# A softmax over heads on one Trainium2 core: six of eight heads copied by ScalarE, two by a DMA of the SyncE queue

## The chip, the core and the metric

The kernel runs on 1 core of one Trainium2 chip. The metric is the device time of the whole program in microseconds, from one launch. The engines that are named below are TensorE (PE), VectorE (DVE), ScalarE (ACT), GpSimd (POOL) and SyncE (SP, which only issues DMAs here).

## The reference

A layer normalisation stands before each of four residual blocks: banded attention, a mixture of experts, attention with its softmax over the heads, and the mixture of experts again, on x of shape (4, 1024, 128). The change lies in the third block:

```python
q = (x @ Wq.T + bq).reshape(B, S, H, D)      # B 4, S 1024, H 16, D 8
k = (x @ Wk.T + bk).reshape(B, S, H, D)
v = (x @ Wv.T + bv).reshape(B, S, H, D)
scores = jnp.einsum('bqnd,bknd->bnqk', q, k) / jnp.sqrt(jnp.float32(D))
attn = jax.nn.softmax(scores, axis=1)        # axis 1 is the head
out = jnp.einsum('bnqk,bknd->bnqd', attn, v)
```

For each pair of a query and a key the 16 exponentials of the heads are added up, and each is divided by that sum.

## The kernel before, in words

The block is the function `head_softmax_attention`. A chunk is 128 queries (4 batches of 8, so 32 chunks), a unit is a chunk against 128 keys (`kt` 0 to 7 in a chunk, so 256 units). In a unit the scores stand with the keys on the 128 partitions, 16 heads x 128 queries along the row; they are made in two halves h of 64 queries each (h0, h1), since each half of all heads fills two PSUM banks of `score`.

For each unit and half: PE makes the scores (`scores_of`, L893); DVE takes the maximum over the heads, negated (`largest`, L1118); PE adds it to the scores (`take_maximum`, L915); ACT takes the exponential into `ex` (L1072), which is a ring of RING = 6 units in SBUF. Only then can PE overwrite that half of `score`.

The sum over 16 heads goes in steps. ACT copies heads 0 to 7 of `ex` into `half` (`copy_heads`, L1035), a ring of SUMS = 4 units. GpSimd issues a DMA that adds heads 8 to 15 onto them (`add_halves`, L847, an accumulating DMA), and when that has landed GpSimd adds four heads to four others (`add_quarters`, L853). PE adds the last four with an identity matrix (`denominator_of`, L925) into `den`. ACT takes the logarithm and exp of its negative, twice (L1041, L1044, L1046). DVE weighs heads 0 to 9 (`weigh`, L1125), GpSimd heads 10 to 15 (`weigh_rest`, L859), and PE multiplies by the values (`attend`, L908), which waits for GpSimd's part only ahead of the 11th head.

The order on each engine is written out by hand. In unit u:
- PE: `take_maximum` h0 of u; `scores_of` h1 of u; `denominator_of` u-4; `scores_of` h0 of u+1; `take_maximum` h1 of u; `attend` u-5; and with even kt a projection or the output product (`ahead`).
- DVE: `largest` h1 of u; `largest` h0 of u+1; `weigh` u-4; and in most units one small operation.
- ACT: exp h0 of u; copy of u-1; the three small ones of u-4; exp h1 of u; with kt 1 and 3 a copy of a projection, with kt 5 that of the output.
- GpSimd, in step u: `add_halves` u-1; `weigh_rest` u-4; `add_quarters` u-2.
- SyncE: once per chunk the queries of the next chunk go to HBM (L804) and come back in another layout in four pieces (L809); in the first three batches so do the keys of the next batch (L814, L816).

Of the kernel before, what the change touches and what calls it, by code (L numbers as in the profile page):

```python
# [21 lines left out]
B, S, E = 4, 1024, 128  # L22
T = B * S
NT = T // P
BT = S // P
# [34 lines left out]
ONE = 1  # L60
# [655 lines left out]
def head_softmax_attention(nc, c, x, mv, ht, q_dram, k_dram, k_first, zero_f16, zero_f32):  # L716
# [6 lines left out]
    NQ = S // P  # L723
    LAST = B * NQ - 1
    LAG, RING, SUMS = 4, 6, 4
    ON_DVE = 10
    BY_DMA = 0
    ALL = B * NQ * BT
    SLABS = range(NH // 4)
    HALVES = S // BLK  # L730
    READS_Q = GH
    xnT, HB, GR, vs = ht.xnT, ht.HB, ht.GR, ht.vs
    with Mem(nc, "head") as m:
# [4 lines left out]
        parts_q, parts_k = m.sb("parts_q", [P, SLOTS, P], F16), m.sb("parts_k", [P, SLOTS, P], F16)  # L738
        parts_first = m.sb("parts_first", [P, HALVES, SLOTS, BLK], F16)
        shift = m.sb("shift", [P, 2, QS], BF16)  # L740
        ex = m.sb("ex", [P, RING, NH, P])
        half = m.sb("half", [P, SUMS, NH // 2, P])
# [6 lines left out]
        k_ready, k_high, k_low = m.sem("k_ready", "pe"), m.sem("k_high", "act"), m.sem("k_low", "dve")  # L749
        q_written, q_placed = m.sem("q_written", "sp"), m.sem("q_placed", "sp")  # L750
        k_written, k_placed = m.sem("k_written", "sp"), m.sem("k_placed", "sp")
        v_ready, v_done = m.sem("v_ready", "pe"), m.sem("v_done", "dve")
        score_ready, shift_ready, shifted = m.sem("score_ready", "pe"), m.sem("shift_ready", "dve"), m.sem("shifted", "pe")
        ex_ready, den_ready = m.sem("ex_ready", "act"), m.sem("den_ready", "pe", 1)
# [3 lines left out]
        av_done, outT_ready = m.sem("av_done", "pe", RING - 1), m.sem("outT_ready", "act")  # L758
        out_ready, added = m.sem("out_ready", "pe"), m.sem("added", "dve")
        summed = [m.sem(f"summed{i}") for i in range(2)]  # L760
        std, rstd = m.sb("std", [P, NT]), m.sb("rstd", [P, NT])
        xn = m.sb("xn", [P, 2, TB, E])
        rstd_chain, std_ready = m.sem("rstd_chain", "dve"), m.sem("std_ready", "act")
# [5 lines left out]
        def exps(unit, h):  # L769

            return 3 * unit + 2 if h == 1 else max(3 * unit, 1)

        def copies(unit):

            return 3 * unit + (4 if unit < ALL - 1 else 3)
# [22 lines left out]
        @block.sync  # L798
        def _(sp):
            m.start(sp, "sp")  # L800

            def place_q(n):
                sp.wait_ge(q_low, ONE + n + 1)
                sp.dma_start(q_dram[:, :, :], parts_q[:, :, :]).then_inc(q_written, 16)  # L804
                sp.wait_ge(q_written, ONE + (n + 1) * 16)
                by_row = q_dram.rearrange("(g r) s c -> (r s) g c", g=NG)
                for n4 in range(GH):
                    rows = slice(n4 * SLOTS * D, (n4 + 1) * SLOTS * D)
                    sp.dma_start(HB[rows, n % 2, n4:NH:GH, :], by_row[rows, :, :]).then_inc(q_placed, 16)  # L809
                sp.wait_ge(q_placed, ONE + (n + 1) * (READS_Q * 16))  # L810

            def place_k(n, buf, kt):
                sp.wait_ge(k_low, ONE + n + 1)
                sp.dma_start(k_dram[:, :, :], parts_k[:, :, :]).then_inc(k_written, 16)  # L814
                sp.wait_ge(k_written, ONE + (n + 1) * 16)
                sp.dma_start(GR[:, buf, :, kt * P:(kt + 1) * P], k_dram.rearrange("(g r) s c -> (r s) g c", g=NG)).then_inc(k_placed, 16)  # L816
                sp.wait_ge(k_placed, ONE + (n + 1) * 16)

            def clear_values(buf):
                sp.dma_start(vs[:, buf * BT:(buf + 1) * BT, :].rearrange("p t s -> p (t s)"), zero_f32.partition_broadcast(P)).then_inc(v_zeroed, 16)  # L820

            sp.dma_start(HB[:, :, :, :].rearrange("p a n q -> p (a n q)"), zero_f16.partition_broadcast(KROWS)).then_inc(q_zeroed, 16)
            clear_values(0)
            for i in range(HALVES):
                sp.wait_ge(k_low, ONE + i + 1)
                sp.dma_start(k_first[i], parts_first[:, i, :, :]).then_inc(k_written, 16)
            sp.wait_ge(k_written, ONE + HALVES * 16)
            for i in range(HALVES):
                sp.dma_start(GR[:, 0, :, i * BLK:(i + 1) * BLK], k_first[i].rearrange("(g r) s c -> (r s) g c", g=NG)).then_inc(k_placed, 16)
            sp.wait_ge(q_zeroed, ONE + 16)  # L830
            place_q(0)
            clear_values(1)
            for b in range(B):
                for q in range(NQ):
                    if b * NQ + q < LAST:
                        place_q(b * NQ + q + 1)
                    if b < B - 1:
                        place_k(HALVES + b * NQ + q, (b + 1) % 2, q)

        @block.gpsimd  # L840
        def _(pool):
            m.start(pool, "pool")

            def add_halves(unit):

                pool.wait_ge(ex_ready, ONE + copies(unit))
                pool.dma_start(half[:, unit % SUMS, :, :], ex[:, unit % RING, 8:16, :], accum_op=ALU.add).then_inc(summed[unit % 2], 16)  # L847

            def add_quarters(unit):

                pool.wait_ge(summed[unit % 2], (unit // 2 + 1) * 16)
                hf = half[:, unit % SUMS, :, :]
                pool.tensor_tensor(hf[:, 0:4, :], hf[:, 0:4, :], hf[:, 4:8, :], ALU.add).then_inc(quarter_ready, 1)  # L853

            def weigh_rest(unit):

                pool.wait_ge(copy_ready, ONE + unit + 1)
                e = ex[:, unit % RING, ON_DVE:NH, :]
                pool.tensor_tensor(e, e, recip[:, unit % 2, :][:, None, :].broadcast_to([P, NH - ON_DVE, P]),  # L859
                                   ALU.mult).then_inc(rest_ready, 1)  # L860

            for step in range(ALL + 1):
                if step > 0:
                    add_halves(step - 1)
                if step >= LAG:
                    weigh_rest(step - LAG)
                if step > 1:
                    add_quarters(step - 2)
            add_quarters(ALL - 1)
            for unit in range(ALL + 1 - LAG, ALL):  # L870
                weigh_rest(unit)
# [145 lines left out]
        def _(act):  # L1017
# [14 lines left out]
            def copy_heads(unit):  # L1032

                act.wait_ge(ex_ready, ONE + exps(unit, 1))
                act.activation(half[:, unit % SUMS, BY_DMA:8, :], ex[:, unit % RING, BY_DMA:8, :], ACT.Copy).then_inc(ex_ready, 1)  # L1035

# [651 lines left out]
def build(nc, drams, x_dram, out):  # L1688
    with ExitStack() as ctx:
        c = {n: ctx.enter_context(nc.sbuf_tensor(f"c_{n}", s, dt)) for n, (s, dt) in SHAPES.items()}  # L1690
        x = ctx.enter_context(nc.sbuf_tensor("x_tokens", [P, NT, E], F32))
        for n in WEIGHTS:
            c[n] = ctx.enter_context(nc.sbuf_tensor(f"c_{n}", [P, WEIGHTS[n], 2, P], F16))
        for att in ("a_", "b_"):
            c[att + "bias"] = ctx.enter_context(nc.sbuf_tensor(f"c_{att}bias", [P, 2], F32))
        c["a_out"] = ctx.enter_context(nc.sbuf_tensor("c_a_out", [P, E], F32))

        mv = ctx.enter_context(nc.sbuf_tensor("moments", [P, NT, 2], F32))
        w_dram = nc.dram_tensor("pair_weights", [NPAIR, 2, T], F32).ap()

        q_dram = nc.dram_tensor("a_queries", [P, SLOTS, QCOLS], F16).ap()
        k_dram = nc.dram_tensor("a_keys", [P, SLOTS, KCOLS], F16).ap()
        v_dram = nc.dram_tensor("a_values", [LEFT + T + VTAIL, E], F32).ap()
        with Mem(nc, "att_a") as m:
            bt = BandTensors(m)
            banded_attention(nc, c, x, mv, bt, q_dram, k_dram, v_dram, x_dram, drams)
        feed_forward(nc, "ffn1", c, x, mv, w_dram, True)
        bq_dram = nc.dram_tensor("b_queries", [P, SLOTS, P], F16).ap()
        bk_dram = nc.dram_tensor("b_keys", [P, SLOTS, P], F16).ap()
        zero_f16, zero_f32 = drams["zero_f16"], drams["zero_f32"][0:BT * (NH + 1) * VSLOT]  # L1710
        bk_first = nc.dram_tensor("b_keys_first", [S // BLK, P, SLOTS, BLK], F16).ap()
        with Mem(nc, "att_b") as m:
            ht = HeadTensors(m)
            head_softmax_attention(nc, c, x, mv, ht, bq_dram, bk_dram, bk_first, zero_f16, zero_f32)
        feed_forward(nc, "ffn2", c, x, mv, w_dram, False, out)
# [72 lines left out]
```

## Time and profile before

| | |
|---|---|
| median of 3 runs | 1930.84 us (1929.66 to 1932.56) |
| the profiled execution | 1932.25 us, of which the span of its instructions is 1930.4 us |
| granted TensorE clock, mean | 0.970 |
| head-softmax block | about 520 to 1622 us of the span; its 256 units from 550.6 (first exponential) to 1604.5 |
| busy in all of the span | PE 95%, DVE 86%, POOL 75%, ACT 74% |

The page tells for each engine how long its instructions were under way. A wait that costs nothing can stand beside an engine that looks idle, so the argument goes by the order of time within one unit and not by the shares.

### The profile page before, as it was taken

The page shows a single profiled execution, that of the slowest core. Times are in us where ns is not written, and L with a number is a line of the kernel's source. Part 1 is how long each engine was busy: PE and PEld are TensorE (multiplying, and loading weights), DVE is VectorE, ACT ScalarE, POOL GpSimd, SP SyncE. Part 2 cuts the span into 40 slices and gives each one's busy share as a digit, 9 for nine tenths or more (in the row PEclk, how much of TensorE's full clock was granted, in tenths as well). Part 3 has the DMA queues.
Part 4 walks back from the last instruction along what each step waited for, and adds up shares of the span by engine and source line. Part 5 has one row for each costly group of instructions (what it writes and reads, how often), then busy time and mean ns, then how long its engine had stood idle before and what let it go on. Part 6 is the DMA issues. An engine that isn't in the chain of part 4 may idle for free. (4 is left out here: it accounts for less than half of the span.)

```text
span 1930.4 us, 52397 instructions
## 1 busy us (share of the span) xinstructions
PE 1826.9 (95%) x20664; PEld 1150.4 (60%) x20664; DVE 1655.3 (86%) x2601; ACT 1425.5 (74%) x2473; POOL 1452.1 (75%) x1180
## 2 busy tenths in 40 slices
PE   5988799999879999999999999999999997999998
PEld 3666644444336666666666666666666666544443
DVE  6766678887679999999999999999999996788776
ACT  4556456666558888888888889888888884566665
POOL 6246256566429999999999999999999997456565
PEclk8999799999979999999999999999999997899999
DMA  6644087767167777777777777777776772868662
GB/s 164 190 107 117 12 152 143 141 128 134 51 163 140 144 135 147 138 142 140 142 138 142 144 137 143 139 142 138 141 136 134 139 137 49 138 152 154 125 126 62
DMA packets 156741, 253.07 MB, mean 131 GB/s; under 512 B 54736, under 2 KB 86368, under 8 KB 155760
## 3 DMA queue, kind: packets, MB, share of 16 engines
q0 software_dynamic: 36864, 134.23, 37.3%
q1 hardware_dynamic: 114112, 112.89, 27.3%
q8 instruction: 164, 2.69, 0.6%
q10 hardware_dynamic: 5520, 2.60, 0.5%
q14 instruction: 81, 0.66, 0.1%
HBM read 96.95 MB, written 18.55 MB: 60 GB/s over the span
## 5 line engine op out<-in xcount | busy, mean ns | idle before, releaser
L1118 DVE TENSOR_REDUCE head_shift<-head_score 128x64 bf16<-128x1024 f32 x512 | 625.9, 1222 | 54.3 <-PE head_score L893 22.4
L1072 ACT ACTIVATE head_ex<-head_score 128x1024 f32<-128x1024 f32 x512 | 519.6, 1015 | 118.0 <-PE head_score L915 117.9
L859 POOL TENSOR_TENSOR head_ex<-head_ex,head_recip 128x768 f32<-128x768 f32 x256 | 551.4, 2154 | 0.2 <-ACT head_recip L1046 0.2
L1374 POOL TENSOR_TENSOR ffn_sw<-ffn_sg,ffn_wide 128x512 f32<-128x512 f32 x256 | 324.4, 1267 | 219.2 <-ACT ffn_sg L1485 204.1
L853 POOL TENSOR_TENSOR head_half<-head_half 128x512 f32<-128x512 f32 x256 | 405.7, 1585 | 0.7 <-DMA head_half<-head_ex 0.7
L1125 DVE TENSOR_TENSOR head_ex<-head_ex,head_recp 128x1280 f32<-128x1280 f32 x256 | 378.2, 1477 | 7.7 <-ACT head_recp L1044 7.7
L915 PE MATMUL head_score<-head_shift,c_identb 128*128 128x512 bf16 x1024 | 312.0, 387 | 19.5 <-DVE head_shift L1118 14.5
L893 PE MATMUL head_score<-att_b_HB,att_b_GR 96*128 96x256 f16 x2048 | 312.2, 275 | 1.9 <-ACT head_ex L1072 1.1
L847 POOL DMA_DIRECT2D head_half<-head_ex x256 | 234.5, 916 | 93.2 <-ACT head_half L1035 85.6
L925 PE MATMUL head_den<-head_half,c_ident 128*128 128x128 f32 x2048 | 272.8, 277 | 5.1 <-POOL head_half L853 4.6
L908 PE MATMUL head_outp<-head_ex,att_b_vs 128*32 128x128 f32 x8192 | 276.7, 276 | 0.0
L908 PEld LDWEIGHTS head_outp<-head_ex,att_b_vs 128*32 128x32 f32 x8192 | 209.6, 110 | 106.8 <-issue 106.5
L1035 ACT ACTIVATE head_half<-head_ex 128x1024 f32<-128x1024 f32 x256 | 268.3, 1048 | 0.0
L1619 DVE TENSOR_TENSOR ffn_hidden<-ffn_sw,ffn_up 128x512 f32<-128x512 f32 x256 | 178.2, 696 | 93.4 <-POOL ffn_sw L1374 86.4
L925 PEld LDWEIGHTS head_den<-head_half,c_ident 128*128 128x128 f32 x2048 | 250.3, 193 | 9.0 <-POOL head_half L853 5.7
L1485 ACT ACTIVATE ffn_sg<-ffn_gate 128x512 f32<-128x512 f32 x272 | 162.1, 596 | 117.2 <-PE ffn_gate L116 116.1
L893 PEld LDWEIGHTS head_score<-att_b_HB,att_b_GR 96*128 96x128 f16 x2048 | 186.4, 98 | 88.6 <-ACT head_ex L1072 43.9
L1490 ACT ACTIVATE ffn_h_parts<-ffn_hidden 128x512 f16<-128x512 f32 x272 | 162.1, 596 | 96.9 <-DVE ffn_hidden L1619 91.4
L1627 DVE TENSOR_TENSOR ffn_h_parts<-ffn_hidden,ffn_h_parts 128x512 f16<-128x512 f32 x272 | 186.0, 684 | 0.1
L915 PEld LDWEIGHTS head_score<-head_shift,c_identb 128*128 128x128 bf16 x1024 | 64.0, 98 | 120.7 <-DVE head_shift L1118 94.7
L114 PE MATMUL ffn_down<-ffn_h_parts,c_down_parts 128*128 128x512 f16 x272 | 103.2, 380 | 3.3 <-DVE ffn_h_parts L1627 3.3
L114 PE MATMUL ffn_up<-ffn_xnT,c_up_parts 128*128 128x512 f16 x272 | 104.2, 383 | 0.6 <-DVE ffn_hidden L1619 0.3
(265 smaller groups left out, 2538.3 us busy)
## 6 DMA issues: line engine op xcount, KB each, us to landing
head_half<-head_ex POOLq DMA_DIRECT2D x256, 512.0 KB, 5.1
ffn_wide<-pair_weights SPq DMA_DIRECT2D x256, 256.0 KB, 9.7
band_v_windows<-a_values SPq DMA_DIRECT2D x24, 192.0 KB, 4.8
att_b_vs<-in_zero_f SPq DMA_DIRECT2D x2, 2176.0 KB, 9.1
a_keys<-band_parts_k SPq DMA_DIRECT2D x12, 295.5 KB, 2.5
att_a_HB<-a_keys SPq DMA_DIRECT2D x48, 73.9 KB
a_queries<-band_parts_q SPq DMA_DIRECT2D x12, 271.5 KB, 2.8
att_a_GR<-a_queries SPq DMA_DIRECT2D x12, 271.5 KB
```

The source lines that it names most:

```text
L847: pool.dma_start(half[:, unit % SUMS, :, :], ex[:, unit % RING, 8:16, :], accum_op=ALU.add).then_inc(summed[unit % 2], 16)
L853: pool.tensor_tensor(hf[:, 0:4, :], hf[:, 0:4, :], hf[:, 4:8, :], ALU.add).then_inc(quarter_ready, 1)
L859: pool.tensor_tensor(e, e, recip[:, unit % 2, :][:, None, :].broadcast_to([P, NH - ON_DVE, P]), ALU.mult).then_inc(rest_ready, 1)
L893: last = pe.matmul(score[:, h, g // 2, (g % 2) * GH * QS:(g % 2 + 1) * GH * QS].rearrange("p (a w) -> p a w", a=GH), GR[:, buf, g, kt * P: ...
L908: last = pe.matmul(outp[g * 32:(g + 1) * 32, 0:P], vs[:, buf * BT + kt, at:at + 32], ex[:, unit % RING, i, :], start=(kt == 0 and n4 == 0) ...
L915: last = pe.matmul(score[:, h, k, :].rearrange("p (a w) -> p a w", a=NH // 2), c["identb"][:, :], shift[:, h, :][:, None, :].broadcast_to( ...
L925: last = pe.matmul(den[:, 0:P], c["ident"][:, :], half[:, unit % SUMS, k, :], start=(i == 0), stop=(i == len(SLABS) - 1))
L1035: act.activation(half[:, unit % SUMS, BY_DMA:8, :], ex[:, unit % RING, BY_DMA:8, :], ACT.Copy).then_inc(ex_ready, 1)
L1072: act.activation(ex[:, unit % RING, :, h * QS:(h + 1) * QS].rearrange("p (a g) w -> p g a w", g=NG), score[:, h, :, :].rearrange("p k (g a ...
L1118: dve.tensor_reduce(shift[:, h, :], score[:, h, :, :].rearrange("p k (a w) -> p w k a", a=NH // 2), AX.XY, ALU.max, negate=True).then_inc( ...
L1125: dve.tensor_tensor(e, e, recp[:, 0:P][:, None, :].broadcast_to([P, ON_DVE, P]), ALU.mult).then_inc(prob_ready, 1)
L1374: pool.tensor_tensor(sw[:, unit % 2, :], sg[:, unit % 2, :], wide[:, k % 2, i, :], ALU.mult).then_inc(sw_ready, 1)
```

## The change

The DMA of the SyncE queue copies heads 0 and 1 of `ex` into `half` (128 partitions x 1 KB), ACT the heads 2 to 7. The DMA waits for the second exponential of its unit, for the DMA of the unit before, and for the denominator that last read the buffer. `add_halves` waits for it (`copied`) beside ACT's copy. SyncE now walks through the units, and the steps for queries and keys are taken apart and put between the copies of certain kt.

```diff
-    BY_DMA = 0
+    BY_DMA = 2
...
+        copied = m.sem("copied", "sp")
...
-            def place_q(n):
+            def copy_heads(unit):
+
+                sp.wait_ge(ex_ready, ONE + exps(unit, 1))
+                sp.wait_ge(copied, ONE + unit * 16)
+                if unit >= SUMS:
+                    sp.wait_ge(den_ready, ONE + 1 + unit - SUMS + 1)
+                sp.dma_start(half[:, unit % SUMS, 0:BY_DMA, :], ex[:, unit % RING, 0:BY_DMA, :]).then_inc(copied, 16)
+
+            def write_q(n):
                 sp.wait_ge(q_low, ONE + n + 1)
                 sp.dma_start(q_dram[:, :, :], parts_q[:, :, :]).then_inc(q_written, 16)
+
+            def place_q(n):
                 sp.wait_ge(q_written, ONE + (n + 1) * 16)
...
-                sp.wait_ge(q_placed, ONE + (n + 1) * (READS_Q * 16))
-
-            def place_k(n, buf, kt):
+
+            def write_k(n):
...
-            for b in range(B):
-                for q in range(NQ):
-                    if b * NQ + q < LAST:
-                        place_q(b * NQ + q + 1)
-                    if b < B - 1:
-                        place_k(HALVES + b * NQ + q, (b + 1) % 2, q)
+            for unit in range(ALL):
+                n, kt = divmod(unit, BT)
+                b, q = divmod(n, NQ)
+                copy_heads(unit)
+                if n < LAST and kt == 1:
+                    sp.wait_ge(q_placed, ONE + (n + 1) * (READS_Q * 16))
+                    write_q(n + 1)
+                if n < LAST and kt == 2:
+                    place_q(n + 1)
+                if b < B - 1 and kt == 4:
+                    sp.wait_ge(k_placed, ONE + (HALVES + n) * 16)
+                    write_k(HALVES + n)
+                if b < B - 1 and kt == 5:
+                    place_k(HALVES + n, (b + 1) % 2, q)
...
                 pool.wait_ge(ex_ready, ONE + copies(unit))
+                pool.wait_ge(copied, ONE + (unit + 1) * 16)
                 pool.dma_start(half[:, unit % SUMS, :, :], ex[:, unit % RING, 8:16, :], accum_op=ALU.add).then_inc(summed[unit % 2], 16)
```

SyncE, in the first chunk of the block, before (the transfers of queries out and back, and of keys out and back):

```order
L820 DMA att_b_vs<-in_zero_f 128x4352
L804 DMA b_queries<-head_parts_q 128x384
L809 DMA att_b_HB<-b_queries 24x4x128 x4
L814 DMA b_keys<-head_parts_k 128x384
L816 DMA att_b_GR<-b_keys 96x4x128
```

and now, the same chunk and the beginning of the next:

```order
L831 DMA att_b_vs<-in_zero_f 128x4352
L809 DMA head_half<-head_ex 128x256 x2
L813 DMA b_queries<-head_parts_q 128x384
L809 DMA head_half<-head_ex 128x256
L820 DMA att_b_HB<-b_queries 24x4x128 x4
L809 DMA head_half<-head_ex 128x256 x2
L824 DMA b_keys<-head_parts_k 128x384
L809 DMA head_half<-head_ex 128x256
L828 DMA att_b_GR<-b_keys 96x4x128
L809 DMA head_half<-head_ex 128x256 x4
```

Eight copies per chunk stand between the five or seven transfers that were there, all in one queue, and none is issued ahead of the exponential of its unit.

GpSimd in the middle of the block, one step, before:

```order
L847 DMA head_half<-head_ex 128x1024 [waits head_ex_ready]
L859 TENSOR_TENSOR head_ex<-head_ex,head_recip 128x768 [waits head_copy_ready]
L853 TENSOR_TENSOR head_half<-head_half 128x512 [waits head_summed1]
```

and now:

```order
L868 DMA head_half<-head_ex 128x1024 [waits head_copied,head_ex_ready]
L880 TENSOR_TENSOR head_ex<-head_ex,head_recip 128x768 [waits head_copy_ready]
L874 TENSOR_TENSOR head_half<-head_half 128x512 [waits head_summed1]
```

Nothing moves there; the issue of the accumulating DMA waits for one semaphore more, and the two operations behind it with it.

## Rows read from the trace of the kernel before

**Rows 1.** Busy time by stretch, 700 to 900 us: PE, PEld, DVE, ACT, POOL, clock, DMA share, GB/s.

```profile
700.00:900.00 200.00, 196.49 (x2586) 136.91 (x2584) 190.80 (x183) 177.34 (x311) 190.72 (x147) 1.00 0.74 141
```

**Rows 2.** Groups by line, 600 to 1300 us: count, busy us, mean ns.

```profile
L1118 DVE TENSOR_REDUCE head_shift<-head_score 128x64 bf16<-128x1024 f32 x339 | 414.5, 1223 | 32.1 <-PE head_score L893 10.5
...
L1035 ACT ACTIVATE head_half<-head_ex 128x1024 f32<-128x1024 f32 x170 | 178.1, 1048 | 0.0
...
L1041 ACT ACTIVATE head_lnd<-head_den 128x128 f32<-128x128 f32 x169 | 45.5, 269 | 0.0
```

**Rows 3.** Timeline from the unit of kt 5: start us, duration us, instruction, [idle before it].

```profile
1001.47 2.56 DVE L1118 TENSOR_REDUCE head_shift<-head_score 128x64 bf16<-128x1024 f32 x2
1001.95 1.05 ACT L1035 ACTIVATE head_half<-head_ex 128x1024 f32<-128x1024 f32 x1
...
1002.75 0.61 PE L915 MATMUL head_score<-head_shift,c_identb 128*128 128x512 bf16 x2
...
1003.29 0.88 POOL L847 DMA_DIRECT2D head_half<-head_ex  x1 [0.33 <-ACT head_half L1035]
...
1003.78 1.00 ACT L1072 ACTIVATE head_ex<-head_score 128x1024 f32<-128x1024 f32 x1
1003.94 1.48 DVE L1125 TENSOR_TENSOR head_ex<-head_ex,head_recp 128x1280 f32<-128x1280 f32 x1
1003.96 2.06 POOL L859 TENSOR_TENSOR head_ex<-head_ex,head_recip 128x768 f32<-128x768 f32 x1
1004.32 0.60 PE L915 MATMUL head_score<-head_shift,c_identb 128*128 128x512 bf16 x2
1004.83 0.61 PE L893 MATMUL head_score<-att_b_HB,att_b_GR 96*128 96x256 f16 x4
...
1005.34 0.28 DVE L1109 SCALAR_TENSOR_TENSOR att_b_vs<-head_proj,c_b_bv 128x128 f32<-128x128 f32 x1
1005.54 2.54 DVE L1118 TENSOR_REDUCE head_shift<-head_score 128x64 bf16<-128x1024 f32 x2
1005.74 1.49 POOL L853 TENSOR_TENSOR head_half<-head_half 128x512 f32<-128x512 f32 x1
...
1007.23 0.88 POOL L847 DMA_DIRECT2D head_half<-head_ex  x1
```

**Rows 4.** The same timeline, further on: attention product and row maximum after kt 6, GpSimd's undisturbed pace.

```profile
1007.54 1.01 ACT L1072 ACTIVATE head_ex<-head_score 128x1024 f32<-128x1024 f32 x1
...
1009.97 2.56 DVE L1118 TENSOR_REDUCE head_shift<-head_score 128x64 bf16<-128x1024 f32 x2 [0.50 <-PE head_score L893]
...
1011.79 1.08 PE L908 MATMUL head_outp<-head_ex,att_b_vs 128*32 128x128 f32 x32
1011.80 0.88 POOL L847 DMA_DIRECT2D head_half<-head_ex  x1 [0.62 <-ACT head_half L1035]
...
1015.71 0.88 POOL L847 DMA_DIRECT2D head_half<-head_ex  x1
```

**Rows 5.** Time to landing, us: the issues of L804 and of L847, each as a whole.

```profile
DMA to landing us min/median/max: 2.3/3.0/4.8
...
DMA to landing us min/median/max: 4.5/5.1/7.1
```

**Rows 6.** Time to landing, us: one L816, issued at 603.4.

```profile
L816 SPq DMA_DIRECT2D att_b_GR<-b_keys x1: 310/310/310, 603.4 to 603.4; - x1
...
DMA to landing us min/median/max: 5.0/5.0/5.0
```

**Rows 7.** Time to landing, us: the L847 issued ahead of that L816.

```profile
L847 POOL DMA_DIRECT2D head_half<-head_ex x1: 880/880/880, 602.5 to 602.5; - x1
...
DMA to landing us min/median/max: 5.7/5.7/5.7
```

**Rows 8.** The last two L847 of the block, in the timeline.

```profile
1602.06 0.88 POOL L847 DMA_DIRECT2D head_half<-head_ex  x1 [0.58 <-ACT head_half L1035]
...
1605.66 1.19 POOL L847 DMA_DIRECT2D head_half<-head_ex  x1
```

More of the change, by code:

```diff
@@ L809, in place_q, with place_k @@
                     sp.dma_start(HB[rows, n % 2, n4:NH:GH, :], by_row[rows, :, :]).then_inc(q_placed, 16)
-                sp.wait_ge(q_placed, ONE + (n + 1) * (READS_Q * 16))
-            def place_k(n, buf, kt):
+            def write_k(n):
                 sp.wait_ge(k_low, ONE + n + 1)
                 sp.dma_start(k_dram[:, :, :], parts_k[:, :, :]).then_inc(k_written, 16)
+            def place_k(n, buf, kt):
                 sp.wait_ge(k_written, ONE + (n + 1) * 16)
                 sp.dma_start(GR[:, buf, :, kt * P:(kt + 1) * P], k_dram.rearrange("(g r) s c -> (r s) g c", g=NG)).then_inc(k_placed, 16)
-                sp.wait_ge(k_placed, ONE + (n + 1) * 16)
             def clear_values(buf):
@@ L830, in _ @@
             sp.wait_ge(q_zeroed, ONE + 16)
+            write_q(0)
             place_q(0)
             clear_values(1)
-            for b in range(B):
-                for q in range(NQ):
-                    if b * NQ + q < LAST:
-                        place_q(b * NQ + q + 1)
-                    if b < B - 1:
-                        place_k(HALVES + b * NQ + q, (b + 1) % 2, q)
+            for unit in range(ALL):
[12 more added lines that the diff above has]
+                    place_k(HALVES + n, (b + 1) % 2, q)
         @block.gpsimd
```

## The prediction

> **What bounds the kernel now.** I first took the busy times of a stretch in the middle of the head-softmax block: in 200 us DVE is busy for 190.8, POOL for 190.7, ACT for 177.3, and the DMA engines for 0.74 of their time, at full TensorE clock [rows 1]. So two engines stand at 95% and the one that the change relieves at 89%. The groups by line give the length of a unit: 339 row maxima in 700 us are 2 per unit, so 700 / 169.5 = 4.13 us [rows 2].
>
> Then I read one unit in order of time [rows 3]. DVE runs without a gap: two maxima from 1001.47, the weighing from 1003.94 until 1005.42, a small one at 1005.34 (neighbours overlap by some 0.1), and the next pair of maxima at 1005.54, which is 4.07 us after the first. Its scores (L893 at 1004.83, 0.61 long) were ready at 1005.44, just in time. Those scores could be written because ACT's second exponential ended at 1003.78 + 1.00 = 4.78; PE began them 0.05 later. PE is one behind the other too: L915, L908, L915, L893. Once per chunk, after kt 6, DVE waits for PE, 0.50 us, because the output product is in PE's row of work [rows 4]. ACT has no part in that wait: it is PE's serial stretch from the maximum of h1 to the scores of h1. So the unit is set by DVE, and after kt 6 by DVE and PE; ACT is a near third at one point, 0.05 us behind.
>
> **What is removed.** ACT's copy takes 1048 ns for 1024 elements a row; an ACT pass over 128 takes 269 ns, hence (1048 - 269) / 896 = 0.87 ns an element [rows 2]. Two heads are 256 elements: 0.22 us less per unit, 256 x 0.22 = 57 us of ACT's time. What of it reaches the end? ACT's second exponential follows its small operations and starts 0.2 to 0.4 us after the L915 that it needs in units like this one (L915 ends at 1003.36, exp at 1003.78 [rows 3]), so it comes up to 0.22 earlier. The scores behind it may start earlier by at most the interval by which they are later than PE alone would have them: in this unit 0.51 us after L915's start, where two passes of 512 columns need about 0.44; 0.07 us. DVE isn't free then: it starts its pair at 1005.54 with the scores there at 1005.44. I count **0** for the gain. Its cover is DVE; if that cover were gone, the gain would be 0.07 in the odd half of the units, 9 us, and the waits of DVE set its outer bound, 0.50 x 31 = 16 us.
>
> **What is added.** SP waits for the second exponential (end of it: I call it E) and issues 128 KB in 1 KB pieces. No row shows an SBUF-to-SBUF copy from SP. The nearest is L804, 96 KB in 768 B pieces from SBUF: 2.3 to 4.8 us to landing, median 3.0 [rows 5]. GpSimd then takes about 0.3 us until it starts (ACT's copy ends at 1003.00, L847 starts at 1003.29 [rows 3]). So the copy is known to GpSimd at E + 0.1 + 2.3 + 0.3 = **E + 2.7** when nothing is in its way, and at E + 5.2 with the largest landing. Before, L847 starts 1007.23 - 1004.78 = 2.45 after E in this unit [rows 3] and 1011.80 - 1008.55 = 3.25 in the next [rows 4]. So a free landing changes nothing.
>
> What can be in its way is the accumulating DMA of the unit before. It lands 4.5 to 7.1 us after its issue, median 5.1 [rows 5], longer than a unit, so it is in flight when the copy is issued unless it is issued later than the copy. An SP transfer issued 0.9 us behind an L847 landed at 603.4 + 5.0 = 608.4 [rows 6], the L847 itself at 602.5 + 5.7 = 608.2 [rows 7]. So it is with 23 of the 24 transfers of L816: they land 0.2 to 0.5 us after their L847, whether issued 0.7 or 3.0 us behind it. So a copy issued **behind** an L847 is taken to land 0.35 us after it: the next L847 then comes 5.1 + 0.35 + 0.3 = 5.75 us after the last. A copy issued **ahead** of it lands freely. The Trainium skill ("DMA: Bandwidth & Descriptors", the section on queues, rings and completion order) says that the semaphore write of a DMA is strongly ordered, behind all earlier writes of the same DMA engine across its queues, and that an engine changes queue only at packet boundaries; by that rule every copy that is behind an accumulating DMA is held until it lands, and without it the sum would keep only the 2 us of the block's end. By that rule, the trace agrees: 608.4 against 608.2.
>
> Now the race. Let x be the time from E to the start of L847. GpSimd's own pace is 1015.71 - 1011.80 = 3.91 us [rows 4] against a mean of 4.13, so undisturbed x falls by 0.2 a unit. The copy of the next unit is issued 4.13 + 0.1 - x after this L847; it collides when that is positive by up to 0.7 (where the boundary is, no row says), so when x has fallen to 3.5 to 4.2. The collision sets x to x - 4.13 + 5.75, up 1.6: **5.1 to 5.8**. Then x falls for six or seven units and collides again: a little over once a chunk, 38 times.
>
> How much x does PE bear? Two things hang on it. (a) `attend` of the unit after next needs L859, which ends 0.6 + 2.1 = 2.7 us after the start of L847. For the L847 that belongs to E = 1004.78 that is the attention product at 1011.79, which waits only ahead of its 11th head, after 20 of 32 passes or 0.67 us: 1012.46 - 2.7 - 1004.78 = 5.0. (b) the denominator needs L853, whose end is 4.0 us after the start of L847 (1007.23 against 1003.29 [rows 3]). Worked through the eight kt of a chunk, (b) allows 4.7 to 5.4. With E earlier by some 0.1, PE bears x to about 4.8 to 5.5, mean 5.1. A peak of 5.1 to 5.8 is over that by 0 to 0.7, and I take the middle, 0.35, because the boundary has no row and both peak and limit vary by unit: 38 x 0.35 = **13 us**, less 3 that DVE hides (0.1 us in odd units, where PE's scores are ready before DVE is). The bounds are 0 and 38 x 0.7 = 27.
>
> **The end of the block.** The last exponential of the block ends about 1603.4, the L847 before the last starts at 1602.06, the last at 1605.66 [rows 8]. Its copy would be issued 1.4 us behind the one before: 5.75 instead of 3.60 us after it. Nothing covers the chain of L847, its landing, L853, denominator and output there: **+2 us**. The beginning has slack (POOL waited there for ACT).
>
> **Moved on SP.** SP issues take 0.3 us each, the four of L809 some 2.6 us; placed after the copy of kt 2, they end about 3 to 4 us after E, before the next E at 4.3 at the latest in all but a few chunks. What they and L813 put in the ring ahead of the copy of kt 3 or 2 is small (24 KB each), and is inside the 2.3 to 4.8 already. Queries have five units until they are wanted. The keys' return now starts at kt 5 and has some 5.3 us until the next batch, three times, against a landing of 3 to 5 us: 0. The DMA share rises: 0.74 of 4.13 is 3.06 us for mostly 512 KB, a quarter of that is 0.76 for the copy, so 0.93 at most; this counts as delay of landings, above.
>
> **Sum.** 0 + (13 - 3) + 2 = +12 us on the profiled execution, 1932.25 to 1944.3. That execution is 1.4 above the median of the runs, 1930.84, so the forecast is **1943**. A measurement of this kernel can tell about 0.2%, 3.9 us, from no change.
>
> **Rivals.**
> - *Hidden.* The copy lands freely because SP's copy needs no HBM, or the boundary lies at 3.5 and PE bears the peak. For it: GpSimd has no wait of weight now and the limits are close to the peaks. Against: the landings of L816 beside L847. Time: 1930.84 + 0 to 2, so 1932. Chance 0.30.
> - *More stalls.* Two collisions a chunk (the transfers of queries add one), each 0.7: 64 x 0.7 = 45, so up to 1976. For: DMA share near 0.93, accumulating DMAs that land in 7.1 instead of 5.1 (L853 wants them within 3.91 + 2.4 = 6.3). Chance 0.11 for 1958 to 1976.
> - *Every copy collides.* Then each unit takes 5.75 us, and 256 x 1.62 = 415 us, 2346. Against: a later L847 falls behind the next copy and ends the collision. Chance 0.03.
> - *Faster.* ACT's exponential, not DVE, holds the scores of h1. Place: L893 at 1004.83, 0.05 after ACT. Price: 9 us with 0.07 in half the units, up to 16. It decides if DVE's gaps (32.1 us in 700 [rows 2]) prove to be waits for scores rather than the cost of its own semaphore between two maxima. Time: 1931 - 9 = 1922. Against: DVE is back to back in odd units. Chance 0.11.
>
> **Numbers.** Forecast case 0.45, time 1943, its own range 1935 (stalls of 0.05) to 1958 (stalls of 0.7). Slower by over 0.2%: 0.45 + 0.11 + 0.03 = 0.59. Within: 0.30. Faster: 0.11. The range 1926 to 1970 leaves out about 0.08 below and 0.08 above.
>
> **What would show it.** L1035's successor at 0.83 us on 768 elements. DVE's idle time ahead of L1118 no smaller. POOL's L868 with waits for the SP copy, about one of every seven of them long, others none; its start 3.5 to 5.8 us after E in place of 2.5 to 3.3. PE idle ahead of the denominator (now L946) or the attention product (now L929) with GpSimd as releaser, some 10 us in all. ACT's idle time up by about 57 us, all of it ahead of L1093. The prediction is wrong if GpSimd waits for the copy in nearly every unit, if PE never waits for GpSimd, or if DVE's gaps shrink.

## The result

The changed kernel takes 1983.18 us in the median of 4 runs (1972.69 to 1992.94), the kernel before 1930.25 us (1929.38 to 1932.56). The ratio is 1.0269, 95% interval 1.0243 to 1.0295: **slower by 2.7%, 53 us**. The direction was forecast, the size wasn't: 1943 was said, and the range ended at 1970. New is the spread as well, 20 us between runs where the kernel before has 3. The profiled execution is the fastest of the four, 1972.69 us with a span of 1970.9, so the trace explains 40 us of the 53.

The page of the changed kernel, by its costliest groups (count | busy us, mean ns | idle before it, releaser), and its two transfers into `half` with the median us to landing:

```profile
L1139 DVE TENSOR_REDUCE head_shift<-head_score 128x64 bf16<-128x1024 f32 x512 | 626.0, 1223 | 95.3 <-PE head_score L914 64.4
L1093 ACT ACTIVATE head_ex<-head_score 128x1024 f32<-128x1024 f32 x512 | 523.0, 1021 | 199.1 <-PE head_score L936 192.5
L880 POOL TENSOR_TENSOR head_ex<-head_ex,head_recip 128x768 f32<-128x768 f32 x256 | 645.1, 2520 | 0.2 <-ACT head_recip L1067 0.2
L874 POOL TENSOR_TENSOR head_half<-head_half 128x512 f32<-128x512 f32 x256 | 498.6, 1948 | 2.1 <-DMA head_half<-head_ex 2.1
...
L868 POOL DMA_DIRECT2D head_half<-head_ex x256 | 328.1, 1282 | 138.0 <-DMA head_half<-head_ex 47.8
...
L929 PE MATMUL head_outp<-head_ex,att_b_vs 128*32 128x128 f32 x8192 | 292.0, 277 | 32.2 <-POOL head_ex L880 32.2
...
L1056 ACT ACTIVATE head_half<-head_ex 128x768 f32<-128x768 f32 x256 | 213.7, 835 | 0.0
...
head_half<-head_ex POOLq DMA_DIRECT2D x256, 512.0 KB, 5.5
...
head_half<-head_ex SPq DMA_DIRECT2D x256, 128.0 KB, 2.6
```

ScalarE's copy is 835 ns for 1048, as computed. ScalarE waits all the longer: the exponential (L1093) has 199.1 us of idle time ahead of it, where it had 118.0. Two lines were not there before. PE stands idle 32.2 us ahead of the attention product (L929) until GpSimd's weighing (L880) ends. And GpSimd's issue of the accumulating DMA (L868) waits 47.8 us for the copy. The maxima on DVE (L1139) went from 54.3 us of idle time to 95.3: PE is late with the scores, and DVE, which set the unit, waits. The same two groups on the page of the kernel before:

```profile
L1118 DVE TENSOR_REDUCE head_shift<-head_score 128x64 bf16<-128x1024 f32 x512 | 625.9, 1222 | 54.3 <-PE head_score L893 22.4
L1072 ACT ACTIVATE head_ex<-head_score 128x1024 f32<-128x1024 f32 x512 | 519.6, 1015 | 118.0 <-PE head_score L915 117.9
```

The stretch 900 to 1100 us of the changed kernel, in the columns of [rows 1]:

```profile
900.00:1100.00 200.00, 190.29 (x2468) 133.11 (x2466) 181.47 (x173) 161.07 (x293) 179.96 (x138) 0.99 0.79 164
```

DVE is busy for 181.5 us of 200 where [rows 1] has 190.8, the DMA engines for 0.79 of their time where they had 0.74. ([rows 1] are those of 700 to 900 us; from 900 to 1100 us the kernel before has 190.9 and 0.74.) The longest stall of all lies in this stretch; from 700 to 900 us the changed kernel has 184.7.

### The profile page after: what moved, and what is told of

It reads as the page before. It is cut to its first block and busy times, and to the rows that moved or that the text cites. A ratio compares the mean times of both kernels' runs of the same rounds, so it can differ in the third digit from the quotient of the medians.

```text
span 1970.9 us, 53166 instructions
## 1 busy us (share of the span) xinstructions
PE 1837.4 (93%) x20664; PEld 1161.0 (59%) x20664; DVE 1657.2 (84%) x2601; ACT 1385.1 (70%) x2473; POOL 1449.9 (74%) x1180
## 5 line engine op out<-in xcount | busy, mean ns | idle before, releaser
L1139 DVE TENSOR_REDUCE head_shift<-head_score 128x64 bf16<-128x1024 f32 x512 | 626.0, 1223 | 95.3 <-PE head_score L914 64.4
L1093 ACT ACTIVATE head_ex<-head_score 128x1024 f32<-128x1024 f32 x512 | 523.0, 1021 | 199.1 <-PE head_score L936 192.5
L880 POOL TENSOR_TENSOR head_ex<-head_ex,head_recip 128x768 f32<-128x768 f32 x256 | 645.1, 2520 | 0.2 <-ACT head_recip L1067 0.2
L874 POOL TENSOR_TENSOR head_half<-head_half 128x512 f32<-128x512 f32 x256 | 498.6, 1948 | 2.1 <-DMA head_half<-head_ex 2.1
L868 POOL DMA_DIRECT2D head_half<-head_ex x256 | 328.1, 1282 | 138.0 <-DMA head_half<-head_ex 47.8
L936 PE MATMUL head_score<-head_shift,c_identb 128*128 128x512 bf16 x1024 | 310.9, 385 | 19.5 <-DVE head_shift L1139 14.0
L929 PE MATMUL head_outp<-head_ex,att_b_vs 128*32 128x128 f32 x8192 | 292.0, 277 | 32.2 <-POOL head_ex L880 32.2
L929 PEld LDWEIGHTS head_outp<-head_ex,att_b_vs 128*32 128x32 f32 x8192 | 214.5, 110 | 148.8 <-issue 106.5
L1056 ACT ACTIVATE head_half<-head_ex 128x768 f32<-128x768 f32 x256 | 213.7, 835 | 0.0
L936 PEld LDWEIGHTS head_score<-head_shift,c_identb 128*128 128x128 bf16 x1024 | 64.1, 97 | 119.0 <-DVE head_shift L1139 95.3
```

What stands on the lines that cost most here:

```text
L929: last = pe.matmul(outp[g * 32:(g + 1) * 32, 0:P], vs[:, buf * BT + kt, at:at + 32], ex[:, unit % RING, i, :], start=(kt == 0 and n4 == 0) ...
L936: last = pe.matmul(score[:, h, k, :].rearrange("p (a w) -> p a w", a=NH // 2), c["identb"][:, :], shift[:, h, :][:, None, :].broadcast_to( ...
L1093: act.activation(ex[:, unit % RING, :, h * QS:(h + 1) * QS].rearrange("p (a g) w -> p g a w", g=NG), score[:, h, :, :].rearrange("p k (g a ...
L1139: dve.tensor_reduce(shift[:, h, :], score[:, h, :, :].rearrange("p k (a w) -> p w k a", a=NH // 2), AX.XY, ALU.max, negate=True).then_inc( ...
```

## Where the time is lost: one collision in the trace

A copy is called held here when it lands with the accumulating DMA of the unit before, which was still in flight when the copy was issued; a stall is a unit that is longer than the median unit of its kt. E and x are as in the prediction: the end of the second exponential of a unit, and the time from E to the start of L868.

The changed kernel's timeline from kt 2 to kt 5 of a chunk (start us, duration us), GpSimd and SyncE:

```profile
1002.20 3.66 SPq L820 DMA_DIRECT2D att_b_HB<-b_queries  x4
1005.97 0.47 SPq L809 DMA_DIRECT2D head_half<-head_ex  x1
```

```profile
1005.47 0.88 POOL L868 DMA_DIRECT2D head_half<-head_ex  x1 [0.27 <-ACT head_ex L1093]
...
1011.22 0.88 POOL L868 DMA_DIRECT2D head_half<-head_ex  x1 [1.79 <-ACT head_ex L1093]
1011.82 2.12 POOL L880 TENSOR_TENSOR head_ex<-head_ex,head_recip 128x768 f32<-128x768 f32 x1
```

The second exponential of kt 3 ends at 1005.24. SyncE is still issuing the four transfers of queries (L820, 3.66 us until 1005.86) and issues the copy at 1005.97, which is 0.50 us behind L868 at 1005.47, the accumulating DMA of kt 2. The landings of the two:

```profile
L809 SPq DMA_DIRECT2D head_half<-head_ex x1: 470/470/470, 1006.0 to 1006.0; - x1
...
DMA to landing us min/median/max: 4.7/4.7/4.7
```

```profile
L868 POOL DMA_DIRECT2D head_half<-head_ex x1: 876/876/876, 1005.5 to 1005.5; - x1
...
DMA to landing us min/median/max: 5.0/5.0/5.0
```

The copy lands at 1010.7, 0.2 us behind the accumulating DMA at 1010.5. The next L868 starts at 1011.22, 5.75 us after the last one. The profile names ACT's exponential as its releaser, with 1.79 us; that one had ended at 1009.35, so it was the copy. The weighing comes at 1011.82, and PE and DVE in the order of time:

```profile
1012.30 0.85 PE L929 MATMUL head_outp<-head_ex,att_b_vs 128*32 128x128 f32 x20
...
1014.00 0.63 PE L929 MATMUL head_outp<-head_ex,att_b_vs 128*32 128x128 f32 x12 [0.85 <-POOL head_ex L880]
...
1014.56 0.60 PE L936 MATMUL head_score<-head_shift,c_identb 128*128 128x512 bf16 x2
...
1015.20 1.02 ACT L1093 ACTIVATE head_ex<-head_score 128x1024 f32<-128x1024 f32 x1 [1.61 <-PE head_score L936]
...
1015.64 1.23 DVE L1139 TENSOR_REDUCE head_shift<-head_score 128x64 bf16<-128x1024 f32 x1 [1.00 <-PE head_score L914]
```

PE does the 20 passes of ten heads at 1012.30, waits 0.85 us for GpSimd's six heads, and everything behind it in PE's row is late: L936, the exponential (1.61 us idle), the maxima (1.00 us idle).

I took E and x for all 256 units of both traces, and put each copy's landing beside that of the accumulating DMA of the unit before:

| | before | after |
|---|---|---|
| end of the second exponential, first unit to last | 1048.6 us | 1091.6 us |
| x, mean | 2.80 us | 4.48 us |
| landing of the accumulating DMA from the start of its record on GpSimd, mean | 5.05 us | 5.56 us |
| the same from the end of that record, mean | 4.14 us | 4.28 us |
| the median unit of each kt, sum over a chunk | 33.0 us | 33.05 us |
| units 5 to 249 that are longer than that median by over 0.15 us | | 37, together 43.1 us |

The undisturbed chunk is as long as it was. The loss, 1091.6 - 1048.6 = 43.0 us, is in these 37 units, which come to 43.1. 36 of them stand two units behind a unit of large x (4.95 us or more): x 5.90 gives 0.86 us, 5.98 gives 1.09, 6.22 gives 1.18, 7.42 gives 2.64. So PE bears an x of 4.5 to 5.0, in the median 4.9 (x less the loss, in 34 of the 37); the largest, 8.41, gives 4.90, more than that limit explains, with three late units in a row. Of the 245 copies of units 5 to 249, 36 land with the accumulating DMA of the unit before (from 0.2 us ahead of it to 0.8 behind), and their x is 5.98 in the mean.

Which copies are held can be told from the records, if the time is taken from the **end** of L868's record. GpSimd's record of an instruction can begin while the one before it still runs. The L868 behind the one at 1011.22:

```profile
1013.60 1.56 POOL L874 TENSOR_TENSOR head_half<-head_half 128x512 f32<-128x512 f32 x1
1014.82 1.18 POOL L868 DMA_DIRECT2D head_half<-head_ex  x1
```

L874 runs until 1015.16; L868's record begins 0.34 us earlier and lasts 1.18 us, where that of a L868 on an idle GpSimd lasts 0.88. From start to start it is 3.60 us behind the last one, from end to end (1012.10 to 1016.00) 3.90. By the end, the copies part cleanly. In the changed kernel 32 of the 245 were issued later than 0.63 us before the end of the L868 of the unit before, and all 32 land behind it, by 0.16 to 0.80 us; of the 198 issued more than 0.68 us before that end, none does; of the 15 in between, two do. (The copy shown, at 1005.97, was issued 0.38 us before the end at 1006.35.) In e3, e4, e5, e6 and e8 below it is the same, 176 of 176 against 0 of 1009, and in e2 243 of 243 against 0 of 2.

## The experiments

Each kernel was timed beside the kernel before on the same chip; the ratio is to that. Four explanations were tried against each other: theory 1, the held copy makes GpSimd late; rival 1, the load on the DMA engines; rival 2, a hold that goes by bytes; and rival 3, SyncE's row of work.

**e1: ScalarE's relief alone.** Heads 0 and 1 are copied by nobody (their place in `half` is set to zero once, by DVE), so the denominators are wrong.

```diff
-                act.activation(half[:, unit % SUMS, BY_DMA:8, :], ex[:, unit % RING, BY_DMA:8, :], ACT.Copy).then_inc(ex_ready, 1)
+                act.activation(half[:, unit % SUMS, 2:8, :], ex[:, unit % RING, 2:8, :], ACT.Copy).then_inc(ex_ready, 1)
```

> The kernel before, in which ScalarE copies heads 2 to 7 only and nobody copies heads 0 and 1 (their place is cleared once; the denominators are wrong). So it is the relief of ScalarE alone. My theory (DVE and PE set the unit, ScalarE is worth nothing): 1930, within 3 us of the kernel before, and DVE's idle time ahead of its maxima stays near 54 us. Rival (ScalarE's second exponential holds the scores of h1): 1915 to 1923.

Measured 1931.25 us, ratio 0.9989 (0.9979 to 0.9999). The two groups of e1 that answer to rows 2:

```profile
L1119 DVE TENSOR_REDUCE head_shift<-head_score 128x64 bf16<-128x1024 f32 x512 | 625.9, 1222 | 55.2 <-PE head_score L893 23.9 <-DVE head_shift L1119 0.5
...
L1072 ACT ACTIVATE head_ex<-head_score 128x1024 f32<-128x1024 f32 x512 | 523.4, 1022 | 155.6 <-PE head_score L915 147.1
```

DVE's idle time is 55.2 us, as before (54.3 on the page); ScalarE's went from 118.0 to 155.6. Relieving ScalarE by 57 us gives about 2 us, by the interval 4 at the most. DVE and PE set the unit.

**e2: the load without the wait.** SyncE moves 128 KB between two spare buffers, ScalarE copies all eight heads, GpSimd doesn't wait.

```diff
-                sp.dma_start(half[:, unit % SUMS, 0:BY_DMA, :], ex[:, unit % RING, 0:BY_DMA, :]).then_inc(copied, 16)
+                sp.dma_start(spare[:, 1, :, :], spare[:, 0, :, :]).then_inc(copied, 16)
...
-                pool.wait_ge(copied, ONE + (unit + 1) * 16)
```

> The changed kernel, with ScalarE copying all eight heads again and the SyncE DMA moving 128 KB between two spare buffers, at the same times; GpSimd does not wait for it. It is the load of the DMA engines and of SyncE's new order alone. Theory 1 (a copy behind an accumulating DMA is held, and GpSimd's wait for it makes PE wait): 1930 to 1938. Rival 1 (the additional 128 KB per unit slow the accumulating DMA and the steps for queries and keys): 1960 or more.

Measured 1933.71 us, ratio 1.0005 (0.9995 to 1.0015). The transfers of e2, median us to landing:

```profile
head_half<-head_ex POOLq DMA_DIRECT2D x256, 512.0 KB, 5.1
...
head_spare<-head_spare SPq DMA_DIRECT2D x256, 128.0 KB, 3.6
```

The accumulating DMA lands in 5.1 us as ever, and the copies, of which 243 of 245 are issued behind one (x stays at 2.8) and land behind it, take 3.6 us in the median. Nobody waits for them, and the time is unchanged. Rival 1 falls: neither the bytes nor SyncE's new order cost anything by themselves.

**e3: the wait without the relief.** e2 with GpSimd's wait put back.

> As e2, and GpSimd waits for the spare copy as it does in the changed kernel. Theory 1: the whole loss is back, 1970 to 1995, since ScalarE's relief was worth nothing; some 35 jumps of L868's start to 5 or more us after the second exponential. Rival 1: the same as e2. If ScalarE's relief was worth something, it is slower than the changed kernel by that.

Measured 1993.44 us, ratio 1.0316 (1.0293 to 1.0338). Three of the waits of e3, 600 to 1300 us:

```profile
PEld head_outp L930 <- POOL head_ex L881: 39.5, 33, 2.5
POOL head_half L869 <- DMA head_spare<-head_spare: 33.5, 17, 3.4
PE head_outp L930 <- POOL head_ex L881: 30.6, 31, 2.2
```

One wait of GpSimd on a semaphore makes the whole loss; what is copied plays no part. 46 copies were held. The ratio is 0.5% above that of the changed kernel. That may be what ScalarE's relief is worth when GpSimd is late, but the two intervals touch (1.0293 and 1.0295), so it isn't shown.

**e4: the same with 8 KB.**

```diff
-                sp.dma_start(spare[:, 1, :, :], spare[:, 0, :, :]).then_inc(copied, 16)
+                sp.dma_start(spare[:, 1, 0, 0:16], spare[:, 0, 0, 0:16]).then_inc(copied, 16)
```

> As e3, with a spare copy of 64 B in a row, 8 KB in all, in place of 128 KB. Theory 1, as far as the hold is one of order (the small copy's semaphore comes behind the accumulating DMA, whatever its size): most of the loss stays, 1955 to 1990. Rival 2 (the hold is one of bytes that queue): the loss goes, 1930 to 1938.

Measured 1975.94 us, ratio 1.0221 (1.0206 to 1.0237). A sixteenth of the bytes keeps 2.2 of the 3.2%. 43 copies land with the accumulating DMA of the unit before. So a small transfer is held as a large one. The bytes make the lesser part, 0.9 of the 3.2%; the accumulating DMA ahead of a held copy lands 4.12 us after the end of its record here, where it took 4.37 in e3.

**e8: one head by the DMA**, `BY_DMA = 1`.

> The changed kernel with one head copied by the DMA (64 KB) and seven by ScalarE. Theory 1 (the hold goes by order, not by bytes): the loss is nearly that of two heads, 1965 to 1990. Rival 2 (bytes): about half of it, 1955 or less.

Measured 1977.34 us, ratio 1.0231 (1.0210 to 1.0252), 41 held. With half the bytes 2.3 of 2.7% are left, and the two intervals overlap. Rival 2 falls with e4 and e8 as the main cause.

**e5: no steps for queries and keys in SyncE's row.** From the second chunk on the scores come from old data.

```diff
-                    write_q(n + 1)
+                    sp.wait_ge(q_low, ONE + n + 2)
+                    sp.sem_inc(q_written, 16)
                 if n < LAST and kt == 2:
-                    place_q(n + 1)
+                    sp.sem_inc(q_placed, READS_Q * 16)
```

(and in the same way for the keys, whose second buffer is filled once ahead of the loop)

> The changed kernel without the transfers of queries and keys from the second chunk on (SyncE keeps the waits and the copies; the scores then come from old data). Theory 1: the stalls that begin with the copy of kt 3 (13 of 36 in the profile) go, the others stay: 1950 to 1970. Rival 3 (the copies are late only because the steps for queries and keys stand in SyncE's row ahead of them): 1930 to 1935.

Measured 1962.95 us, ratio 1.0164 (1.0130 to 1.0197), with runs from 1958.97 to 1971.24. 32 copies are still held, now none at kt 3, where the changed kernel had 13 of its 36. So about 1.0%, 20 us, comes from the transfers that stand in the row (directly, and by the larger peaks), and 1.6% is there without them. Rival 3 explains a part.

**e6: one unit more of lag.** `LAG, RING, SUMS = 5, 7, 5` in the changed kernel.

> The changed kernel with the weighing and the denominator one unit later (LAG 5, ring of exponentials 7, of sums 5). GpSimd may then be some 4.1 us later before PE waits for it. Theory 1: jumps of L868 to 5 to 8 us stay and cost nothing, 1930 to 1940. Rival 1 (the engines are slower under the load of the DMAs): 1965 to 1990, as the changed kernel.

Measured 1976.49 us, ratio 1.0232 (1.0217 to 1.0247): the expectation failed. The group of e6 that tells why:

```profile
L931 PE MATMUL head_outp<-head_ex,att_b_vs 128*32 128x128 f32 x8192 | 294.5, 277 | 32.2 <-POOL head_ex L882 32.0
```

The time lies in the range that was said for rival 1, but the trace shows the other cause: PE waits for the weighing (32.0 us) as in the changed kernel. LAG moves `weigh_rest` (u - LAG) and `attend` (u - LAG - 1) together, so the time between them stays one unit; only the denominator got room. The design was at fault: of my two limits, (a) is the one that holds.

**e7: the control**, the same LAG in the kernel before.

> The kernel before with the same LAG 5, the control to e6. Theory: no engine waited for GpSimd before, so 1930 to 1936 (the block's end is a little longer).

Measured 1931.96 us, ratio 1.0000 (0.9990 to 1.0009).

**e9: room where it is wanted.** e6, and GpSimd's step in another order:

```diff
             for step in range(ALL + 1):
-                if step > 0:
-                    add_halves(step - 1)
                 if step >= LAG:
                     weigh_rest(step - LAG)
-                if step > 1:
-                    add_quarters(step - 2)
+                if step > 2:
+                    add_quarters(step - 3)
+                if step > 0:
+                    add_halves(step - 1)
+            add_quarters(ALL - 2)
```

> The changed kernel with room for a late GpSimd. LAG 5 as in e6, which by itself gave the attention product no room, since the weighing and the product that waits for it moved together; so here GpSimd's step is also put in another order: weigh_rest of u-5, add_quarters of u-3, add_halves of u-1. What waits for the copy now stands last in the step, L868 is issued some 6.6 us after the second exponential, and the product has 2.4 us in hand. Theory 1: 1930 to 1938, PE waits for GpSimd hardly at all, while the copies are still issued behind an accumulating DMA. Rival 1 (something else in the changed kernel costs the time): 1960 or more.

Measured 1934.60 us, ratio 1.0016 (1.0005 to 1.0026). Two of the waits of e9, 600 to 1300 us, GpSimd's and DVE's longest:

```profile
POOL head_ex L882 <- ACT head_recip L1070: 39.4, 101, 0.8
...
DVE head_shift L1142 <- PE head_score L917: 11.0, 22, 0.5
```

The issue of the accumulating DMA now starts 5.9 to 6.6 us after E, 1.1 us or more after its copy has landed, so it doesn't wait for the copy; PE doesn't wait for GpSimd at all. All the same the copies are held: 202 of 245 land within a microsecond behind the accumulating DMA issued two units earlier, the others later, none ahead of it. Units longer than their median come to 0.7 us in all. The same copy with the same hold costs nothing where GpSimd reaches the wait late in its step and PE has a unit more of lag. That settles the cause: not the transfer, not its bytes, but what is queued behind the wait.

**e11: its control**, the same order without a DMA copy.

> The kernel before with the same LAG and order, the control to e9. Theory: 1930 to 1938, no gain since GpSimd was not waited for.

Measured 1936.04 us, ratio 1.0023 (1.0014 to 1.0033). Against it e9 is 0.07% faster, with intervals that overlap: ScalarE's relief is worth nothing that these runs can tell.

**e12 and e13: DVE relieved by a head**, `ON_DVE = 9` in e11 and in e9, to look for a version that beats both kernels.

> e11 with head 9 weighed by GpSimd instead of DVE: 1477 / 10 = 148 ns less for DVE per unit, 2130 / 6 = 355 ns more for GpSimd. My reading that DVE sets the units with odd kt: 128 x 0.14 = 18 us less, 1912 to 1918, if GpSimd's own pace is the 3.60 us that it showed when it was late in the changed kernel (3.60 + 0.36 = 3.96). Rival (its pace is 3.91 us as in the kernel before): 4.27 us a unit, 1960 or more.

> e9 with head 9 weighed by GpSimd. As e12, and if DVE is relieved ScalarE's relief may count: 1908 to 1918. Rival (GpSimd's pace 3.91 us, or its waits for the copy back): 1960 or more.

Measured 1956.55 us, ratio 1.0129 (1.0114 to 1.0144), and 1955.84 us, ratio 1.0125 (1.0110 to 1.0140). The groups of GpSimd and of DVE's maxima in e12, 600 to 1300 us:

```profile
L861 POOL TENSOR_TENSOR head_ex<-head_ex,head_recip 128x896 f32<-128x896 f32 x167 | 676.4, 4077 | 0.0
L855 POOL TENSOR_TENSOR head_half<-head_half 128x512 f32<-128x512 f32 x168 | 527.5, 3140 | 0.0
L849 POOL DMA_DIRECT2D head_half<-head_ex x168 | 463.6, 2760 | 0.0
L1121 DVE TENSOR_REDUCE head_shift<-head_score 128x64 bf16<-128x1024 f32 x335 | 410.0, 1224 | 58.6 <-PE head_score L896 39.1
```

Two issues of the accumulating DMA in a row, from e12's timeline:

```profile
1001.22 2.98 POOL L849 DMA_DIRECT2D head_half<-head_ex  x1
...
1005.48 2.90 POOL L849 DMA_DIRECT2D head_half<-head_ex  x1
```

GpSimd has no idle time at all and is the bound. The records of its three instructions overlap, so their mean times are no pace; their ends tell it. These two are 4.18 us apart (1004.20, 1008.38), and in units 5 to 249 all are 4.17 to 4.22. In the changed kernel the ends are 3.91 us apart while GpSimd catches up, the pace of the kernel before [rows 4]; the seventh head adds 0.28. So the rival of e12 and e13 had the cause right, a pace of 3.91 us; it asked 0.08 too much for the head, and its 1960 is 4 us too long. The 3.60 on which I had counted is a distance of record starts. No version was found that beats the kernel before.

## Why the prediction was wrong, step by step

- *The bound and the gain of 0*: right. e1 gives 0.9989, and e9 against e11 nothing that can be told.
- *A copy issued behind an accumulating DMA lands with it*: right, and the boundary for which there was no row is a sharp one, 0.63 us before the end of L868's record. Counted from the start of the record it looks like a rule with exceptions: 98 of 245 copies were issued over 0.25 us behind that start, and 62 of them weren't held. All 62 were issued at least 0.63 us before the end.
- *About 38 stalls*: 37. GpSimd catches up at the 3.91 us a unit that was read from [rows 4]: behind each of the 36 held copies the next end of an L868 follows after 3.89 to 3.93 us.
- *The peak of x, 5.1 to 5.8*: **the term that failed**. I took 5.1 + 0.35 + 0.3 = 5.75 us from one L868 to the next over a held copy, from an x of 3.5 to 4.2 before it and a unit of 4.13, in the middle 5.47. Measured over the 36, from start to start: 5.90 until the accumulating DMA has landed, the copy 0.23 behind it, GpSimd's start 0.65 after that, in sum 6.78; from an x of 3.47 and a unit of 4.27 that gives 5.98. 0.61 us of the 6.78 is only the record of the first L868 beginning early, and it is missing from the 3.47. With the end of the record less 0.88 as the start, it is 4.08 + 5.28 + 0.23 + 0.65 - 4.27. So the jump is 6.16 where 5.75 was said, and the largest part of that is GpSimd's start behind a landed copy, 0.65 for 0.30; x ahead of the jump is 4.08 where the middle was 3.85.
- *What PE bears, 4.8 to 5.5, mean 5.1*: 4.5 to 5.0, median 4.9. With the peak 0.5 higher and the limit 0.2 to 0.3 lower, a stall is 43.1 / 37 = 1.16 us where 0.35 was said. Where peak and limit lie that close, errors of half a microsecond and less make a factor of three in the loss.
- *Moved on SP: 0*: wrong by some 20 us (e5). I had put the four transfers' 2.6 us of issue before the next E "in all but a few chunks"; they took 3.66 in the unit shown (2.4 in the median of the changed kernel), and a copy issued late is issued behind L868, which is the very case that matters. Part of these 20 us acts by way of the peaks (the held copies of e5 have an x of 5.78 in the mean, for 5.98), so it doesn't simply add to the term above.
- *The block's end, +2*: 0. The last two L868 start 3.60 us apart as before.
- *"Hidden" (0.30)* and *"faster" (0.11)* did not come. *"More stalls"* (0.11) is what happened in size, though by larger and not by more stalls, and 1983 lies above its 1976 too. *"Every copy collides"* did not come, for the reason given: the late L868 falls behind the next copy.
- *What the profile would show*: GpSimd's long waits in one unit of seven, PE idle with GpSimd as releaser, ScalarE's idle time ahead of its exponential: as said. DVE's gaps grew, which I hadn't listed.

The Trainium skill ("DMA: Bandwidth & Descriptors", queues, rings and completion order) has the semaphore write of a DMA behind earlier writes of its engine across queues. By that rule a small copy is held like a large one, and the trace agrees in the 43 held copies of 8 KB (e4). Counted from the end of L868's record, the traces of the changed kernel and of e2 to e6 and e8 agree with it in all 451 copies issued later than 0.63 us before that end.

## What to carry to other kernels

Work moved from an engine with slack to a DMA saves nothing and adds a wait; price that wait by what is queued behind the waiting instruction and how late the engine at the bound can bear it, not by the transfer's median. If a small transfer must be waited for while a larger one of another queue is in flight, count it as landing with the larger one, and put the wait last in its engine's step, with a unit more of lag behind it: together that turned +2.7% into +0.2%, where the lag alone left +2.3%. Where the margin is under a microsecond, measure the delay of the start behind a landed DMA by itself before trusting a sum. And take GpSimd's pace, and the moment of its DMA, from the ends of its records: when it is behind, the starts come early.

## What the runs showed of the hardware that I had not expected

- A copy of 8 KB in flight beside an accumulating DMA of 512 KB is held until that lands about as often (43 of 245) as one of 128 KB (36, and 46 in e3).
- Whether a copy is held goes by 0.63 us before the end of the record of the DMA ahead of it: of the copies issued later, 451 of 451 landed behind that DMA; of those issued more than 0.68 us before the end, none of 1209 did (changed kernel, e2 to e6, e8).
- GpSimd's records begin early when it is behind: L868 lasts 1.28 us in the mean of the changed kernel and 0.92 in the kernel before, L849 up to 3.1 in e12. So a landing counted from the start looks late: 62 of 256 are over 6.05 us, against 2 before, with 5.04 us from the end of the record in the mean of the 62 and 4.28 in that of all.
- GpSimd starts 0.54 us after a held copy has landed (30 of the 36; four 0.83, two 1.9), where it started 0.3 us after ScalarE's copy.
- GpSimd's three instructions of a unit take 3.91 us from end to end when nothing is waited for, 4.19 with a seventh head (e12).

Open: why 72 copies that were not held took 2.9 to 4.7 us to land, where the median of the free ones is 2.4; and two units in which L868 started 1.9 us after its held copy had landed (x 8.41 and 7.42). No run was made on these. That the medians lie 10 us above the profiled run is put down to more such stalls, but only the profiled runs have a trace, so this is argued and not shown.
